# Two cross-attentions: bf16 score products of 99 rows become float32r products on half the array, with other banks and another order

## What is computed

```python
qh, kh, vh = split_heads(q @ wq.T + bq), split_heads(k @ wk.T + bk), split_heads(v @ wv.T + bv)   # 16 heads of 16
scores = einsum('bhqd,bhkd->bhqk', qh, kh) / 4          # masked keys at -1e9
out = einsum('bhqk,bhkd->bhqd', softmax(scores), vh)    # 512 queries, 1024 keys
return merge(out) @ wo.T + bo
```

## Time and profile before

| | us |
|---|---|
| median of 3 runs | 981.42 (981.02 to 981.84) |
| the profiled execution | 979.4, span 977.6 |
| loop of the first cross-attention (first T to last exponential) | 180.5 to 377.5 |
| loop of the second | 733.8 to 838.7 |
| busy in the span: PE, PE weight load, DVE, ACT, POOL | 882.1, 485.2, 667.6, 501.1, 335.0 |

### The profile page before, as it was taken

The page is one execution under the profiler, slowest core; times in us unless marked ns, Lnnn a source line. Parts: engine busy times, 40 slices in busy tenths (PEclk is TensorE's granted clock), DMA queues, the critical chain, the costliest instruction groups (busy, mean ns, idle before and its releaser), DMA issues. The chain is left out here.

```text
span 977.6 us, 13423 instructions
## 1 busy us (share of the span) xinstructions
PE 882.1 (90%) x4318; PEld 485.2 (50%) x4318; DVE 667.6 (68%) x1371; ACT 501.1 (51%) x996; POOL 335.0 (34%) x340
## 2 busy tenths in 40 slices
PE   5889998999999998699989999998989999769996
PEld 2345553433332324366657888786433322434575
DVE  5865677888889944445558777875699996545654
ACT  3876544677777783012126565553207778243321
POOL 7335636400000001146567665563320000126833
PEclk9989998999999999599999999999999999969999
DMA  5040017122213810753240000000201450075200
GB/s 158 1 159 3 1 36 118 19 51 51 43 43 61 297 54 1 274 229 119 98 119 1 1 1 1 1 1 1 82 3 30 189 195 1 1 296 170 69 17 27
DMA packets 41656, 73.81 MB, mean 76 GB/s; under 512 B 8964, under 2 KB 27780, under 8 KB 40436
## 3 DMA queue, kind: packets, MB, share of 16 engines
q1 hardware_dynamic: 36372, 59.68, 20.1%
q0 software_dynamic: 4400, 13.11, 4.2%
q10 hardware_dynamic: 816, 0.17, 0.1%
HBM read 49.67 MB, written 10.49 MB: 62 GB/s over the span
## 5 line engine op out<-in xcount | busy, mean ns | idle before, releaser
L1081 DVE TENSOR_REDUCE c_amx<-PS 128x1 f32<-128x512 f32 x256 | 159.1, 683 | 27.6 <-PE PS L981 27.3
L1174 ACT ACTIVATE c_aE<-PS 128x512 f32<-128x512 f32 x256 | 132.6, 602 | 47.1 <-PE PS L993 46.9
L1880 POOL TENSOR_SCALAR s_Pn<-s_Pr,s_rs 128x512 f32<-128x512 f32 x64 | 100.3, 1568 | 56.5 <-DVE s_rs L1922 56.4
L72 POOL TENSOR_SCALAR rstd<-mv 128x4 f32<-128x4 f32 x8 | 1.9, 232 | 336.7 <-DVE mv L95 336.6
L981 PE MATMUL PS<-c_aKs,c_aQs 99*128 99x512 bf16 x256 | 96.5, 388 | 5.1 <-DMA c_aQs<-area 3.6
L993 PE MATMUL PS<-c_aQs,c_aKs 99*128 99x512 bf16 x256 | 94.5, 380 | 3.5 <-ACT c_aE L1174 2.3
L1081 DVE TENSOR_REDUCE h_amx<-PS 128x1 f32<-128x512 f32 x128 | 79.6, 683 | 8.6 <-PE PS L981 8.3
L1174 ACT ACTIVATE h_aE<-PS 128x512 f32<-128x512 f32 x128 | 67.6, 600 | 21.6 <-PE PS L993 21.3
L2018 ACT ACTIVATE s_Pr<-PS,s_nmx 128x512 f32<-128x512 f32 x64 | 44.2, 690 | 65.5 <-DVE s_nmx L1915 65.5
L1004 PE MATMUL PS<-c_aE,c_VB 128*17 128x512 f32 x512 | 67.4, 598 | 0.1
L981 PEld LDWEIGHTS PS<-c_aKs,c_aQs 99*128 99x128 bf16 x256 | 24.9, 98 | 79.0 <-DVE c_amx L1081 55.4
(11 more groups left out here) (486 smaller groups left out, 1957.3 us busy)
## 6 DMA issues: line engine op xcount, KB each, us to landing
area<-in_e_w SPq DMA_DIRECT2D x16, 512.0 KB, 9.8
area<-in_g_w SPq DMA_DIRECT2D x8, 1024.0 KB, 6.2
c_aKs<-area SPq DMA_DIRECT2D x48, 128.0 KB
g_B<-in_g_b SPq DMA_DIRECT2D x1, 4096.0 KB, 13.9
c_aQs<-area SPq DMA_DIRECT2D x48, 64.0 KB
h_aQs<-h_QP SPq DMA_DIRECT2D x48, 64.0 KB
early<-in_ctxT SPq DMA_DIRECT2D x2, 1024.0 KB, 7.3
e_B<-in_e_b SPq DMA_DIRECT2D x1, 2048.0 KB
```

What stands on the lines that cost most here:

```text
L1081: dve.tensor_reduce(self.mx[:, qt, j, half:half + 1], PS[:, n % MB, :], AX.X, ALU.max).then_inc(self.max_done, 1)
L1174: act.activation(self.E[kt % 2][:, j, :], PS[:, MB + x % XB, :], ACT.Exp, scale=0.25).then_inc(self.exp_done, 1)
L1880: pool.tensor_scalar(Pn[g % NPB][:, :], Pr[g % NPB][:, :], rs[:, g % NPB:g % NPB + 1], None, ALU.mult).then_inc(pn_ready, 1)
```

## The change

Queries and keys are cut into two float32r pieces instead of three bf16 pieces; three slots of 16 rows hold the three products that matter, and with three rows ahead of them a product contracts over 51 rows. Heads 0 and 2 lie on partitions 0 to 50, heads 1 and 3 on 64 to 114. The order on PE is S of head x, then T of head x ^ 1, so each such pair uses both halves of the array.

S rotates over four banks, T over three; the transposes of outputs take a turn among the first, those of the maxima, late value tiles and second found keys ("specials", "extras") a turn among the second. Values, transposes and `during` move from the end of a step to behind its third pair (BEFORE = 3). Scores for the maxima run three steps ahead instead of one (AHEAD = 3). The maxima's transposes are copied once, by ScalarE, into a tile MTs, and SyncE places their rows by four DMAs (`tails`). Late value tiles come one at a time at steps 2 and 4. In the second attention ScalarE issues one expert load in each unit at step 2, instead of SyncE two in each of four. The ring of banks for the projections before the loop (RING) has four banks instead of five.

```diff
-NBLK = 6
-TAIL = NBLK * HD
+NBLK = 3
 TAIL_ROWS = 3
-ROWS = TAIL + TAIL_ROWS
+HALF = P // 2
+ROWS = TAIL_ROWS + NBLK * HD
...
+def rows_of_head(j):
+    return slice(j % 2 * HALF, j % 2 * HALF + ROWS)
...
-MB, XB = 3, 3
+MB, XB, VALUE_BANK = 4, 3, 6
+AHEAD = 3
+BEFORE = 3
...
-        self.Qs = [sb(f"Qs{n}", [ROWS, GH, S], BF16) for n in range(NQ)]
-        self.Ks = [sb(f"Ks{n}", [ROWS, KH, NK], BF16) for n in range(NKB)]
+        self.Qs = [sb(f"Qs{n}", [P, PAIRS_H, S], F32R) for n in range(NQ)]
+        self.Ks = [sb(f"Ks{n}", [P, self.KP, NK], F32R) for n in range(NKB)]
...
-        n = (u + 1) * self.C + kt + 1
+        n = (u + 1) * self.C + kt + AHEAD
...
-        for u in range(2, UNITS):
-            if u >= 3:
-                sp.wait_ge(self.av_done, (u - 2) * self.KT)
-            load(u, u % 3)
+        for u in range(UNITS):
+            self.tails(sp, u)
+            if u + 2 < UNITS:
+                if u >= 1:
+                    sp.wait_ge(self.st_done, u * self.KT * GH)
+                load(u + 2, (u + 2) % 3)
+
+    def tails(self, sp, u):
+
+        sp.wait_ge(self.t_copied, u + 1)
+        for j in range(GH):
+            sp.dma_start(self.Qs[u % self.NQ][tail_of_head(j), j // 2, :].bitcast(F32),
+                         self.MTs[32 * j:32 * j + TAIL_ROWS, :].bitcast(F32)).then_inc(self.tails_in, 16)
...
+        def transposed_scores(u, kt, x):
+
+            n = (u * KT + kt) * GH + x
+            j = x ^ 1
+            r = rows_of_head(j)
+            if kt == 0 and x == 0:
+                pe.wait_ge(self.tails_in, 16 * GH * (u + 1))
+            item = self.exp_item(n)
+            self.wait_exp_bank(pe, item)
+            pe.matmul(self.exp_bank(item), self.Ks[self.key_buffer(u)][r, j // 2 % self.KP, kt * P:(kt + 1) * P],
+                      self.Qs[u % self.NQ][r, j // 2, :], start=True, stop=True).then_inc(self.st_done, 1)
...
                 for j in range(GH):
+                    if j == BEFORE:
+                        if kt == KT - AHEAD and u + 1 < UNITS:
+                            maxima_transposes(u + 1)
+                        if during:
+                            during(pe, u, kt)
+                        if kt > 0:
+                            values(u, kt - 1)
+                        elif u > 0:
+                            values(u - 1, KT - 1)
+                        if kt == 1 and u > 0:
+                            output_transposes(u - 1)
                     if v is not None:
                         scores(v, c, j)
                     transposed_scores(u, kt, j)
...
-        def upper_tails(u):
-            dve.wait_ge(self.mT_done, u + 1)
...
-        def tails(u):
+        def copy_maxima(u):
             act.wait_ge(self.mT_done, u + 1)
...
+            act.activation(self.MTs[:, :], self.exp_bank(self.special_item("m", u)).bitcast(BF16)[:, 0:S],
+                           ACT.Copy).then_inc(self.t_copied, 1)
...
-    RING = (6, 5, 3, 4, 7)
+    RING = (6, 5, 3, 4)
...
-KEY_SLOTS = ((0, 3, 5), (1, 4), (2,))
-QUERY_SLOTS = ((0, 1, 2), (3, 4), (5,))
+KEY_SLOTS = ((0, 1), (2,))
+QUERY_SLOTS = ((0, 2), (1,))
+LATE_STEPS = (2, 4)
...
-                if u >= NQ:
-                    for e in range(2 * (u - NQ), 2 * (u - NQ + 1)):
-                        sh.weights[1].load_expert(sp, e)
...
-                if (u, kt) == (0, 2):
+                if (u, kt) == (1, 2):
                     take_keys(1)
...
+                if kt == 2:
+                    sh.weights[1].load_expert(act, u)
```

More of the change, by code:

```diff
@@ new lines, in special_item, with max_bank, exp_bank, wait_max_bank @@
+    def special_item(self, what, i):
+        return next(at + n for n, (at, w, k) in enumerate(self.specials) if (w, k) == (what, i))
+    def max_bank(self, item):
+        return self.PS[:, self.max_banks[item % MB], :]
+    def exp_bank(self, item):
+        return self.PS[:, self.exp_banks[item % XB], :]
+    def wait_max_bank(self, pe, item):
+        before = item - MB
+        if before < 0:
+            return
+        for u in range(UNITS):
+            if self.out_item(u) == before:
+                pe.wait_ge(self.o_normed, u + 1)
+                return
+        pe.wait_ge(self.max_done, before + 1 - sum(self.out_item(u) < before for u in range(UNITS)))
@@ new lines, in wait_exp_bank @@
+    def wait_exp_bank(self, pe, item):
+        before = item - XB
+        if before < 0:
+            return
+        for at, what, i in self.specials:
+            if self.special_item(what, i) == before:
+                if what == "m":
+                    pe.wait_ge(self.t_copied, i + 1)
+                else:
+                    self.extra_free(pe, i)
+                return
+        pe.wait_ge(self.exp_done, before + 1 - sum(self.special_item(w, i) < before for _, w, i in self.specials))
@@ L1039, in step @@
                     transposed_scores(u, kt, j)
[L1040 to L1051, removed]
                 if u == UNITS - 1:
                     meanwhile(pe, kt, KT)
-        for c in range(C + 1):
+        for c in range(C + AHEAD):
             for j in range(GH):
@@ L1125, in step @@
                 if v is not None:
-                    maxima(v, c)
+                    maxima(v, c, range(BEFORE))
+                if kt == 1 and u > 0:
+                    normalise(u - 1)
+                if v is not None:
+                    maxima(v, c, range(BEFORE, GH))
                     if c == C - 1:
                         negated(v)
[L1129 to L1132, removed]
                 if during:
@@ L1140, in vector @@
         negated(0)
[L1141 to L1144, removed]
+        for c in range(AHEAD):
+            maxima(1, c)
         for u in range(UNITS):
@@ L1396, in cross_stage @@
     VB = sb("VB", [P, UNITS, KT, GH, VW])
-    loads = 1 + sum(map(len, KEY_SLOTS)) + 1 + sum(map(len, QUERY_SLOTS))
-    at = Attention(nc, ctx, stage, PS, "c_a", NK, GH, sh.ident, sh.identb, loads)
+    loads = 2 * (1 + sum(map(len, KEY_SLOTS)) + 1 + sum(map(len, QUERY_SLOTS)))
+    at = Attention(nc, ctx, stage, PS, "c_a", NK, GH, sh.ident, sh.identb, loads, (0, 1, 2, 7), (3, 4, 5),
+                   extras=[(u, kt) for u in range(UNITS // B) for kt in LATE_STEPS])
     at.V = VB
@@ L1445, in part, with rounded @@
         return QP[p][:, m, b * S:(b + 1) * S]
+    def rounded(what, n, p):
+        return part(what, n, p).bitcast(F32R)
     def value_rows(t):
@@ L1665, in late_values @@
             def late_values(act, u, kt):
-                if kt == 4 and u < UNITS // B:
-                    for t in range(KT + VLATE * u, KT + VLATE * (u + 1)):
-                        take_values(t)
+                if late_tile(u, kt) is not None:
+                    take_values(late_tile(u, kt))
             at.scalar(act, during=late_values)
```

384 lines of the change are left out of this document (181 added, 203 removed).

## The result

The kernel after takes 998.19 us (median of four, 994.66 to 999.09) against 981.63 of the kernel before on the same chip: ratio 1.0164, 95% interval [1.0137, 1.0191]. It is slower by 1.6%; forecast were 965 us and faster. The profiled execution is the quickest of the four, 994.66, span 992.8. Against the span of before that is 15.2 more, where the forecast had 16.0 less: 31.2 to explain.

The account below looks back on a forecast made before the run. PE was taken to bound both loops at 2.80 us a step. Gains of 12.4 (first loop) and 5.6 (second) less 2.0 (DVE) made 16.0: 979.4 to 963.4, median 2.0 above, 965 us; range 947 to 985.

Parts of the forecast that it names:

- The pairs: Both loops: S and T on the two row halves run side by side, 0.23 us a pair, PE's step 2.00.
- the ring: Both loops: exponential, T, values, T, exponential through three exponential banks sets the step, 2.53 us (bounds 2.38 and 2.66).
- the start of the first loop: Before the first loop: first T at 183.5 us instead of 180.5, bounds 182.5 and 185; first S costs another 0.5.
- the rows in the second loop: Second loop's unit starts: maxima's rows land 0 to 1.5 us late in each of four units, 1.4 in all.
- the specials: Each loop: transposes of maxima and outputs add 14 sets at 0.49 us, 6.9.
- the clock: Second loop's start: a step of 2.00 at half speed costs 2.0 us more; lower clock inside the loops a danger.
- halves do not run together: Rival, 13%, both loops: row halves do not overlap, step 2.955 us, total 1003, slower.
- loads wait on their own half: Rival, 8%, both loops: weight loads wait for matmuls on their own rows, pair 0.41, PE's step 2.72, total 983 us.
- DVE's overlap: Both loops: DVE's limit close to the ring costs 0.15 us in each of 13 units, 2.0, bounds 0 and 5.
- late tiles: First loop: one late value tile in each of eight steps, about 1.0 us each, 8.0 in all.
- SyncE's queue: Rival, 12%: 20 SyncE issues a unit instead of 14 make loads or tails late in both loops, total 977 us.
- Expert loads by ScalarE: Second loop: each takes about 0.45 us of ScalarE's queue, covered by waiting in the ring, so cost 0.

Follow-up runs that it names:

- the first four experiments: Single edits of the kernel after: maxima's rows copied by engines, 988.26 us; unit 1's constant rows later, 992.94; second-loop loads behind rows, 1000.90; expert loads in units 6 and 7, 997.31.
- Projections behind four S: Kernel after with the first loop's preparation placing projections behind each chunk's four S instead of behind each two: 995.38 us, ratio 1.0136.

## Why the prediction was wrong

The pairs and the ring came as forecast in kind. Two steps failed: the start of the first loop, forecast 3.5 later and measured 10.7 later, where the constant rows that SyncE issues ahead of the first S were put at nothing and the issues of the maxima's rows too low; and the rows in the second loop, forecast 1.4 and measured 8.7. The ring, the specials and the clock were terms that came out too small.

**Pairs: right.** 0.23 forecast, 0.22 to 0.24 measured (0.34 right behind the values), and the rivals *halves do not run together* and *loads wait on their own half* are refuted, though the time came out near the first one's 1003: another cause, the same number. The Trainium skill's rule ("TensorE: Matmul & The Clock Gate", Part 3, The mechanism), a load overlaps only where the row group differs, does not hold in this trace; the same section also allows a load into a background weight buffer:

```profile
323.45 0.19 PEld L1073 LDWEIGHTS PS<-c_aKs,c_aQs 51*128 51x128 f32 x1
```

This load is for the S of head 0, on partitions 0 to 50, and it lies inside the T of head 2 (323.34 to 323.83), which is on the same half.

**The ring: right mechanism, 2.62 for 2.53.** The values and the way from exponential to T cost what the earlier trace rows said within 0.01; T to exponential took 0.56 for 0.42 and T to values 0.42 for 0.32, as a matmul whose load begins no more than 0.01 before it takes 0.49 to 0.50 and not 0.38 to 0.39 (I had put 0.08 for each, it is 0.11). 96 x 0.09 = 8.6 of the 31.2. Nothing shows DVE's overlap, 2.0: the ring is longer.

**Specials: mis-sized.** I had two sets of transposes at 0.49 in a unit. In the first loop they cost 0.86 (step 1, with values waiting 0.20 for ScalarE's copy of the outputs) and 0.68 (step 5); in the second both fall into step 1 and the maxima's wait for the bank of that step's first exponential:

```profile
793.24 0.38 PE L1108 MATMUL PS<-identb,h_aMT 128*128 128x128 bf16 x4 [0.58 <-ACT h_aE L1261]
```

That step took 4.17, 1.55 more than a plain one. Some 3.9 and 3.2; late tiles 1.13 for 1.0, another 1.0.

**The start: wrong in path and price.** The first S, forecast 0.5 later, came 3.9 later. I counted loads but not what SyncE issues ahead of them: eight constant-row transfers, 6.0 us (before: four, 2.4), of which moving four won 3.2. The first T, forecast 183.5 and with the later S 184.0, came at 191.2. I had put the maxima's transposes at 178.5; they came at 186.09, from the late first S and a preparation in which two S and their projection take 1.49, not 1.29. The four issues took 2.85, not 1.1: a transfer from a 3-row tile in SBUF costs SyncE 0.71, and the 0.27 of the earlier trace rows is one from another source. Landing was shorter than assumed, 1.2. And eight S of the chunks ahead stand between transposes and T; I checked that VectorE's end did not stand in the way of 183.5, not what the order costs once the start slips. Two chunks instead of three won 2.9 there.

**Waits in the second loop: 8.7, not 1.4.** The term named the expert load in the same DMA engines, at 0 to 1.5 in each of four units, and the rival *SyncE's queue* the place; the expert load beside the rows is the reason, and the queue mostly not, since the waits went with the loads while SyncE's order stayed. From last issue to T it is 3.8 us (799.14 to 802.94) there, and 1.2 (190.0 to 191.2) where next to nothing else moves (DMA share 0.04 from 188 to 192). Expert loads by ScalarE cost its queue nothing, as forecast (0.55 each, hidden); they cost the DMA engines.

**The clock: named as a danger, not priced in the first loop.** Waiting S at the first loop's start brought the level down to 1.2 GHz: unit 0 took 26.84 for 23.1 at full clock, 3.7. In the second I had counted 2.0, for one step; in after the low clock also follows the waits at unit starts. What it costs differs between executions: unit 0 of the first loop took 24.45 in one run of the same order, and unit 0 of the second 13.25 in after but 15.96 to 16.02 in the first four experiments and in *Projections behind four S*.

Together, ring, VectorE, specials with late tiles, start (first S, then first S to first T), clock and waits: 8.6 − 2.0 + 8.1 + 3.4 + 3.8 + 3.7 + 7.3 = 32.9 against 31.2; with 1.8 between the loops and −1.6 behind them, whose cause I did not test, 33.1. The parts overlap a little: the low clock is in the waits and in the steps.

## What to carry to other kernels

Before work is moved off a bound engine, write out the ring through each rotating buffer: producer, consumer, release, and everything that the producer's engine does between two uses of that buffer; its length, not the engine's sum, is the next floor, and moving work inside the ring does not shorten it. Price what a change adds ahead of a loop (order, issues, work that must run before the first product) as carefully as the loop itself: here the first loop gained 2.6 and the way to its first T lost 10.7. A small transfer that a critical wait depends on should not share the DMA engines with a bulk load; here copying it with an idle engine was worth 10. And run a kernel several times before a difference of a few microseconds at a stage is given a cause.

## What the hardware showed that was not expected

Float32r matmuls on the two row halves run together, 0.22 to 0.24 a pair, where on the full array a single one takes 0.24. A value group of two heads takes 0.97, one of four 0.99. A float32r matmul of 512 columns whose load could not run ahead takes 0.49 to 0.50, 0.11 longer. A transfer from a 3-row SBUF tile costs SyncE 0.71 to issue, and T could start 1.2 after the last issue where next to nothing else moved and 3.8 after it beside an expert load. Idle matmuls kept PE's clock at 1.00 at the start of the first loop, but ahead of the second it fell beside them. And taking work from PE can cost time: without most value matmuls the mean granted clock fell from 0.942 to 0.856, and the kernel took about 14 longer with less to do.
